# A delta-rule walk that deals its side work unevenly over the levels of each inverse

## The chip, the core and the metric

One core of a Trainium2 chip runs the whole program. Its five engines, TensorE (PE), VectorE (DVE), ScalarE (ACT), GpSimd (POOL) and SyncE (SP), each take their own instructions in the order in which the program issued them, and wait for one another on semaphores. The metric is device time in microseconds (us); lower is better.

## The reference

The program computes four blocks on 8 sequences of 512 tokens of width 256; two of them (a normalised linear attention, and a grouped attention with a mixture of experts) come in a later part of the program, and the tree-routed feed-forward partly so. The change touches only the first block, a gated delta rule with 8 heads, key width 128 and value width 64:

```python
def step(state, inp):
    q_t, k_t, v_t, a_t, b_t = inp
    retained = jnp.einsum('bhvk,bhk->bhv', state, k_t)
    a4 = a_t[..., None, None]
    b4 = b_t[..., None, None]
    rk = retained[..., None] * k_t[:, :, None, :]
    vk = v_t[..., None] * k_t[:, :, None, :]
    state = a4 * (state - b4 * rk) + b4 * vk
    o_t = jnp.einsum('bhvk,bhk->bhv', state, q_t)
    return (state, o_t)
...
q = _causal_dw_conv_silu(x @ Wq, conv_q).reshape(bsz, seq_len, H, KD)
k = _causal_dw_conv_silu(x @ Wk, conv_k).reshape(bsz, seq_len, H, KD)
v = _causal_dw_conv_silu(x @ Wv, conv_v).reshape(bsz, seq_len, H, VD)
q = _l2norm(q)
k = _l2norm(k)
...
_, outT = jax.lax.scan(step, state0, (qT, kT, vT, aT, bT))
...
out = out * rms * o_norm_w * jax.nn.silu(gate)
```

Instead of 512 steps one after another, the kernel works on chunks of 128 tokens. The steps inside a chunk amount to the inverse of a unit triangular 128x128 matrix for each head; the state is then carried from chunk to chunk.

## The kernel before

**Calls and inversions.** The stage `Delta` has 16 calls (`CALLS`): 8 sequences, and for each of them two groups of 4 heads. A call n has four chunks t = 0 to 3. Their inverses are made in two pairs, `invert(e, n, 0)` for chunks 0 and 1, and `invert(e, n, 1)` for chunks 2 and 3. That gives 32 inversions, m = 2n + pair; below an *even* inversion is the first of a call and an *odd* one the second.

**The generators.** Each engine walks the same list of generators. Each `yield` ends a step, and a step may issue nothing on an engine.

- `invert` has 30 steps, called M0 to M29 here. M0 to M5 are the set-up: PE makes K·K and K·Q (L708, L717), DVE scales them with the decays (L759, L764), DVE and ACT cut out the diagonal blocks (L901, L850), and DVE makes the first block inverse (L906, L909, L911). Then come six levels of 4 steps each, M6 to M29. In a level, PE makes the product T (L796; L798 in level 5; L820 with the transposes L824 in level 6). ACT copies it to SBUF (TB, L857). PE makes Z from it (L809; L834 in level 6). DVE merges Z into the inverse (L919) and transposes it (L921), and only then can the next T start. In level 6, DVE copies the results out (L929, L933). T stands at M6, M10, M14, M18, M22 and M26, Z two steps behind each, the copies TB at M7, M11, M15, M19, M23, M27, and L919 at M9, M13, M17, M21. From level 3 on PE also gets products that nobody reads, L841, one or two in each gap.
- `project` has 50 steps, p0 to p49, and works for the next call. Ten items (v for two halves, then k and q for four heads) stand at p2, p4, ..., p20 on PE: two fp32 matmuls of 512 columns (L570; the profile lists each as two records). One step later ACT copies the first tap of the convolution (L615), and another step later DVE adds the other three taps (L663, three instructions). Two Silu (L620) follow on ACT at p7, p11, p15, p19 and p23. Items alternate between two PSUM banks, so item j on PE waits for the three taps of item j - 2. p22 and p24 make the gate (L579 on PE, L625 on ACT; the second waits for the Silu of the first), p26 and p28 turn v (L589, L630), p30 to p44 turn k and q (L599 on PE, squares L641 on ACT, L669 on DVE).
- `state` carries the state over two chunks, 6 steps each: QS (L968 and L970 on PE), then L1004 to L1011 on DVE, then Uh (L977), L1015, O1 (L984 and L986), L1020 and L1021. The second pair adds 6 steps that normalise the output (L1026 to L1034 on DVE, a square root L1046 on ACT, L1063 and L1068 on POOL). `last` is the state of the previous call's second pair, `here` that of this call's first.
- `beside` is the routing of the feed-forward: small steps on all engines (L1282 to L1480) that share the walk.

**The dealing.** `side_by_side` issues one step of the inverse, and then as many steps of each other generator as its rate has added up to:

```python
def side_by_side(main, *others):
    due = [0.0] * len(others)
    for _ in main:
        for j, (steps, rate) in enumerate(others):
            due[j] += rate
            while due[j] >= 1:
                next(steps, None)
                due[j] -= 1
```

The rates are numbers written by hand in `walk`. `(next(main) for _ in range(6))` covers the set-up, and the bare `main` that follows covers all six levels. ACT has one table for Exp, one for Silu and one for Sqrt; where another function is wanted, an ACT_TABLE_LOAD goes ahead.

## Time and profile before

| | us |
|---|---|
| median of 3 runs | 3632.18 (3629.6 to 3633.38) |
| the profiled execution, time | 3636.05 |
| its span | 3634.3 |
| of it before the first inversion | 145 |
| from the first inversion's start to its last product | 1666 |
| PE busy in the span | 3184.9 (88%) |
| mean granted TensorE clock | 0.914 |

The span is from the first instruction of the profile to the last. The time of the profiled execution is 1.75 us longer than its span and 3.87 us above the median. A granted clock of 1.00 is the upper of TensorE's two levels (2.4 GHz) and 0.50 the lower (1.2 GHz), so a mean of 0.9 over a stretch says that a fifth of it was at the lower one.

### The profile page before, as it was taken

The numbers are of one execution on the slowest core, as the hardware profiler recorded it, in microseconds if no ns is written. First come the engines' busy times: TensorE is split into PE (matmuls) and PEld (weight loads), VectorE is DVE, ScalarE is ACT, GpSimd is POOL, SyncE is SP. The second block draws the span as 40 slices with busy tenths as digits, with TensorE's granted clock in tenths as the row PEclk, the third lists the DMA queues.
The fourth block names the chain that finished last, engine by engine and source line by source line (L and its number), as shares of the span: only waits on it lengthen the run. The fifth ranks groups of instructions, "written<-read, shape, count | busy, mean of one in ns | idle before, by whom it ended". The sixth has DMA issues, their size and how long they took to land.

```text
span 3634.3 us, 86956 instructions
## 1 busy us (share of the span) xinstructions
PE 3184.9 (88%) x35518; PEld 2222.1 (61%) x35518; DVE 2190.0 (60%) x4820; ACT 1428.4 (39%) x3328; POOL 933.8 (26%) x851
## 2 busy tenths in 40 slices
PE   5689988888998888888868889776999999999998
PEld 5366766666766666666757767665545554554553
DVE  6566778666678676678346645635445545545444
ACT  1544444444444444344136622134433433433341
POOL 0112231412222412221405536331221221220110
PEclk7799988899898999998679999988989999999999
DMA  6101211302111301111347755384111111111000
GB/s 239 41 34 49 65 48 34 126 27 65 54 47 49 120 26 50 60 54 32 101 152 198 188 161 145 102 276 157 24 43 45 47 35 47 40 31 41 1 18 18
DMA packets 224087, 280.89 MB, mean 77 GB/s; under 512 B 35072, under 2 KB 172464, under 8 KB 223312
## 3 DMA queue, kind: packets, MB, share of 16 engines
q1 hardware_dynamic: 184448, 216.93, 18.5%
q0 software_dynamic: 34896, 54.20, 6.7%
q8 instruction: 288, 4.72, 0.5%
q10 hardware_dynamic: 4352, 4.20, 0.3%
q14 instruction: 103, 0.84, 0.1%
HBM read 184.64 MB, written 90.62 MB: 76 GB/s over the span
## 4 chain that ended last, share of the span: by engine, by line
PE 68%; DVE 16%; ACT 5%; issue 4%; DMA 3%; POOL 1%; DVEq 0%; ACTq 0%; SPq 0%; POOLq 0%
PE banks L3024 6%; PE banks L570 5%; DVE s_d_kq L663 3%; PE banks L2590 3%; PE banks L809 3%; PE banks L2574 2%; PE banks L1940 2%; PE banks L1282 2%; PE banks L1949 2%; PE banks L796 2%; PE banks L2602 2%; PE banks L970 2%; PE banks L2832 2%; PE banks L968 2%; PE banks L2742 2%
## 5 line engine op out<-in xcount | busy, mean ns | idle before, releaser
L570 PE MATMUL banks<-s_d_xT,s_w_qkvg 128*128 128x512 f32 x640 | 349.1, 674 | 14.7 <-DVE s_d_kq L663 9.5
L663 DVE SCALAR_TENSOR_TENSOR s_d_kq<-banks,s_conv_w,s_d_kq 128x511 f32<-128x511 f32 (+2 forms) x384 | 286.0, 745 | 51.2 <-ACT s_d_kq L615 41.6
L2704 ACT ACTIVATE s_g_pT<-banks 128x1536 f32<-128x1536 f32 (+1 forms) x96 | 152.8, 1591 | 359.7 <-PE banks L2592 359.7
L2668 DVE TENSOR_REDUCE s_g_nmax<-banks 128x4 f32<-128x512 f32 (+3 forms) x128 | 188.0, 1490 | 161.2 <-PE banks L2576 161.2
L3024 PE MATMUL banks<-s_m_we,s_m_tT 128*128 128x512 f32 x512 | 233.9, 602 | 8.5 <-DVE s_m_x L3088 8.2
L641 ACT ACTIVATE s_d_square<-banks 128x128 bf16<-128x128 f32 x512 | 134.1, 276 | 168.6 <-PE banks L599 168.5
L570 PEld LDWEIGHTS banks<-s_d_xT,s_w_qkvg 128*128 128x128 f32 x640 | 126.7, 212 | 118.6 <-issue 91.2
L615 ACT ACTIVATE s_d_kq<-banks,s_conv_w 128x512 f32<-128x512 f32 x128 | 87.8, 686 | 275.6 <-PE banks L570 274.9
L1940 PE MATMUL banks<-s_q_xsT,s_q_w 128*128 x1008 | 159.1, 281 | 37.4 <-issue 28.2
L1940 PEld LDWEIGHTS banks<-s_q_xsT,s_q_w 128*128 128x128 f32 x1008 | 153.0, 195 | 59.5 <-issue 47.6
L796 PEld LDWEIGHTS banks<-s_d_Xc,s_d_Mc 32*32 32x32 f32 x8192 | 94.4, 117 | 125.4 <-DVE s_d_Xc L909 55.8
L809 PE MATMUL banks<-s_d_TB,s_d_XT 32*32 32x32 f32 x9216 | 131.0, 203 | 40.2 <-ACT s_d_TB L857 37.7
L796 PE MATMUL banks<-s_d_Xc,s_d_Mc 32*32 32x32 f32 x8192 | 110.4, 206 | 63.4 <-DVE s_d_Xc L909 48.9
L809 PEld LDWEIGHTS banks<-s_d_TB,s_d_XT 32*32 32x32 f32 x9216 | 111.7, 115 | 88.0 <-issue 42.4
L3024 PEld LDWEIGHTS banks<-s_m_we,s_m_tT 128*128 128x128 f32 x512 | 93.5, 192 | 112.9 <-issue 99.5
L1949 PE MATMUL banks<-s_q_w,s_q_hm 128*128 (+1 forms) x504 | 157.5, 395 | 3.6 <-DVE s_q_hm L2000 2.9
L1215 POOL DMA_INDIRECT s_r_bias<-b,s_r_leafi x96 | 94.3, 982 | 201.7 <-DMA tree<-s_r_bias 95.8
L2000 DVE SCALAR_TENSOR_TENSOR s_q_hm<-s_q_lrow,s_q_w,s_q_hT 128x128 f32<-128x128 f32 x252 | 86.6, 344 | 93.0 <-ACT s_q_hT L1970 78.5
L1970 ACT ACTIVATE s_q_hT<-banks,s_q_w 128x128 f32<-128x128 f32 x252 | 92.2, 366 | 118.0 <-PE banks L1940 115.3
L919 DVE COPY_PREDICATED s_d_Xc<-c_mask,banks 128x256 f32<-128x256 uint32 x128 | 56.4, 441 | 131.3 <-PE banks L809 131.3
L2029 POOL DMA_INDIRECT tree<-s_q_acc,s_q_toki x64 | 102.3, 1599 | 111.2 <-DVE s_q_acc L2009 94.7
L3086 DVE SCALAR_TENSOR_TENSOR s_m_x<-banks,s_m_comb,s_m_x 128x256 f32<-128x256 f32 x128 | 61.8, 483 | 108.0 <-PE banks L3024 105.7
(411 smaller groups left out, 7620.9 us busy)
## 6 DMA issues: line engine op xcount, KB each, us to landing
s_q_w<-w12p SPq DMA_DIRECT2D x128, 257.0 KB, 5.9
s_q_xs<-xs SPq DMA_DIRECT2D x32, 516.0 KB, 5.6
s_d_E<-sums SPq DMA_DIRECT2D x64, 256.0 KB, 3.5
s_r_xT<-xfT SPq DMA_DIRECT2D x12, 1024.0 KB
tree<-s_r_bias SPq DMA_DIRECT2D x96, 128.0 KB, 2.6
s_r_work<-xf SPq DMA_DIRECT2D x24, 512.0 KB, 4.1
og<-s_d_o SPq DMA_DIRECT2D x16, 512.0 KB, 3.0
sorted<-s_q_acc SPq DMA_DIRECT2D x32, 256.0 KB, 2.1
```

The source lines that it names most:

```text
L570: ins = e.matmul(bk[6 + j % 2][:], w[:, par, c, self.COL[what] + h * P:self.COL[what] + (h + 1) * P], xT[:, c, :], start=(c == 0), stop=(c ...
L641: ins = e.activation(self.square[:, k, h, :], bk[7 - k][:, h * P:(h + 1) * P], ACT.Square, accum_out=self.sums[:, k, H * t + h:H * t + h + 1])
L663: e.scalar_tensor_tensor(d[:, a:], bk[6 + j % 2][:, 0:SEQ - a], cw[:, par, k0 + 3 - a:k0 + 4 - a], d[:, a:], ALU.mult, ALU.add).then_inc(s ...
L796: ins = e.matmul(bk[0][r, 32 * a:32 * a + 32], Mc[r, a, :], Xc[r, a, :], start=True, stop=True)
L809: ins = e.matmul(bk[2][r, 32 * a:32 * a + 32], XT[r, a, :], TB[r, a, :], start=True, stop=True)
L1940: ins = e.matmul(bk[Q % 3][:, 0:P], self.w1[Q % self.COPIES][:, c * P:(c + 1) * P], tiles[:, c, ds(at[Q], 1), :], start=(c == 0), stop=(c ...
L1949: e.matmul(bk[3 + q % 3][:, 0:DIM], self.hm[q % 4][:], self.w12[:, ds(self.group(q, at[q]), 1), 258:], start=True, stop=True).then_inc(sel ...
L2029: e.indirect_dma_start(self.g.dram[f"tree{F}"], bass.IndirectOffsetOnAxis(self.toki[F % 2][:, t:t + 1].bitcast(U32), 0), self.acc[:, t * D ...
L2590: ins = e.matmul(bk[k][:, a:a + SEQ - c * P], qkT[32 * k:32 * k + 17, 4, c * P:(c + 1) * P], qkT[32 * k:32 * k + 17, j, c * P:SEQ], start= ...
L2668: e.tensor_reduce(self.nmax[:, t, :].rearrange("p (k d) -> p k d", k=4)[:, :, 16], psum[:, 0:4, a:a + (t + 1) * P], AX.X, ALU.max, negate= ...
L2704: e.activation(self.pT[c][:], psum[:, 0:4, 0:self.COLUMNS[c]], ACT.Exp).then_inc(self.exped, 1)
L3024: ins = e.matmul(bk[q][:], tT[:, c, t * P:(t + 1) * P], self.we[:, c, (2 * half + q) * 512:(2 * half + q + 1) * 512], start=(c == 0), stop ...
```

## The change

The six levels are split after the third. In an even inversion `last` gets 0.9 of a step per step of the inverse in levels 1 to 3 and 0.4 in levels 4 to 6 (0.64 throughout before), and `ahead`, the next projections, 0.5 and then 1.2 (0.8 throughout before). In an odd inversion `here` gets 0.7 and then 0.35 (0.5 before), and `ahead` 0.5 and 1.2 (0.8 before). Neither `beside` nor the set-up changes its rate.

```diff
             main, here = invert(e, n, 0), state(e, n, 0)
             side_by_side((next(main) for _ in range(6)), (last, 0.5), (ahead, 0.67))
-            side_by_side(main, (last, 0.64), (ahead, 0.8), (beside, 0.62))
+            side_by_side((next(main) for _ in range(12)), (last, 0.9), (ahead, 0.5), (beside, 0.62))
+            side_by_side(main, (last, 0.4), (ahead, 1.2), (beside, 0.62))
             finish(last)
             main = invert(e, n, 1)
             side_by_side((next(main) for _ in range(6)), (ahead, 1.34))
-            side_by_side(main, (here, 0.5), (ahead, 0.8), (beside, 0.62))
+            side_by_side((next(main) for _ in range(12)), (here, 0.7), (ahead, 0.5), (beside, 0.62))
+            side_by_side(main, (here, 0.35), (ahead, 1.2), (beside, 0.62))
             finish(here, ahead)
```

In levels 1 to 3 of an even inversion stood project's p4 to p12 and steps 3 to 9 of `last`; now p4 to p9 and steps 3 to 12. In levels 4 to 6 stood p13 to p22 and the rest of `last`; now p10 to p23 and steps 13 to 16. The last item that has its taps added ahead of L933 was p20's; now it is p22's. An odd inversion starts one step of `project` later, at p24. All engines keep the same instructions but for ACT's table loads: the program has 46 of them at L620 before and 32 after. The changed file has two lines more ahead of the routing, so that L1282 is L1284 there.

ScalarE, levels 1 to 3 of the even inversion m = 18; L857 is the copy TB that the next Z waits for, L615 a first tap, L620 a Silu. Before:

```order
L857 ACTIVATE s_d_TB<-banks 128x256
L615 ACTIVATE s_d_vT<-banks,s_conv_w 128x512
L615 ACTIVATE s_d_kq<-banks,s_conv_w 128x512
L620 ACT_TABLE_LOAD
L620 ACTIVATE s_d_vT<-s_d_vT 128x512 x2
L857 ACTIVATE s_d_TB<-banks 128x256
L615 ACTIVATE s_d_kq<-banks,s_conv_w 128x512
L857 ACTIVATE s_d_TB<-banks 128x256
```

After:

```order
L857 ACTIVATE s_d_TB<-banks 128x256
L615 ACTIVATE s_d_vT<-banks,s_conv_w 128x512
L857 ACTIVATE s_d_TB<-banks 128x256
L615 ACTIVATE s_d_kq<-banks,s_conv_w 128x512
L620 ACT_TABLE_LOAD
L620 ACTIVATE s_d_vT<-s_d_vT 128x512 x2
L857 ACTIVATE s_d_TB<-banks 128x256
L615 ACTIVATE s_d_kq<-banks,s_conv_w 128x512
```

The first tap of item 2, the table load and the Silu of v stood ahead of level 2's copy and now stand behind it.

TensorE at the same place, from the T of level 2 (L796) to the T of level 3; L809 is Z, L968 with L970 is QS, L977 is Uh, L570 an item. Before:

```order
L796 MATMUL banks<-s_d_Xc,s_d_Mc 32x32 x32
L809 MATMUL banks<-s_d_TB,s_d_XT 32x32 x32
L968 MATMUL banks<-s_d_S,s_d_kq 128x64 x4
L970 MATMUL banks<-s_d_S,s_d_kq 128x64 x4
L570 MATMUL banks<-s_d_xT,s_w_qkvg 128x512 x2
L796 MATMUL banks<-s_d_Xc,s_d_Mc 32x32 x32
```

After:

```order
L796 MATMUL banks<-s_d_Xc,s_d_Mc 32x32 x32
L968 MATMUL banks<-s_d_S,s_d_kq 128x64 x4
L970 MATMUL banks<-s_d_S,s_d_kq 128x64 x4
L570 MATMUL banks<-s_d_xT,s_w_qkvg 128x512 x2
L809 MATMUL banks<-s_d_TB,s_d_XT 32x32 x32
L977 MATMUL banks<-s_d_R,s_d_Pf 128x64 x4
L796 MATMUL banks<-s_d_Xc,s_d_Mc 32x32 x32
```

Between T and Z of level 2 stood nothing; QS and an item now stand there, and only Uh stands behind Z.

VectorE at the end of level 6 of the same inversion; L663 are the taps (three instructions to an item), L929 and L933 copy the finished inverse, and L933 lets PE go on with the next set-up. Before:

```order
L929 COPY s_d_Pf<-banks 128x512
L663 SCALAR_TENSOR_TENSOR s_d_kq<-banks,s_conv_w,s_d_kq 128x511
L663 SCALAR_TENSOR_TENSOR s_d_kq<-banks,s_conv_w,s_d_kq 128x510
L663 SCALAR_TENSOR_TENSOR s_d_kq<-banks,s_conv_w,s_d_kq 128x509
L1394 TENSOR_SCALAR s_r_posi<-s_r_pos 128x32
L933 COPY s_d_Pf<-banks 64x8x64
```

After:

```order
L929 COPY s_d_Pf<-banks 128x512
L663 SCALAR_TENSOR_TENSOR s_d_kq<-banks,s_conv_w,s_d_kq 128x511
L663 SCALAR_TENSOR_TENSOR s_d_kq<-banks,s_conv_w,s_d_kq 128x510
L663 SCALAR_TENSOR_TENSOR s_d_kq<-banks,s_conv_w,s_d_kq 128x509
L1393 TENSOR_REDUCE s_r_pos<-s_r_work 128x32
L663 SCALAR_TENSOR_TENSOR s_d_kq<-banks,s_conv_w,s_d_kq 128x511
L663 SCALAR_TENSOR_TENSOR s_d_kq<-banks,s_conv_w,s_d_kq 128x510
L663 SCALAR_TENSOR_TENSOR s_d_kq<-banks,s_conv_w,s_d_kq 128x509
L933 COPY s_d_Pf<-banks 64x8x64
```

The taps of the last item moved from behind L933 to ahead of it. From level 3's L919 to L933 DVE has the taps of seven items now, and had those of five.

## Rows read from the trace of the kernel before

**Rows 1.** The page: its first line and the first of part 1.
```profile
span 3634.3 us, 86956 instructions
...
PE 3184.9 (88%) x35518; PEld 2222.1 (61%) x35518; DVE 2190.0 (60%) x4820; ACT 1428.4 (39%) x3328; POOL 933.8 (26%) x851
```

**Rows 2.** Busy time by stretch: the delta stage (stretch, length, engines, clock, DMA).
```profile
145.00:1811.00 1666.00, 1473.00 (x24880) 1106.38 (x24879) 1158.56 (x2462) 712.64 (x1953) 448.00 (x430) 0.89 0.19 57
```

**Rows 3.** Waits of PE in the delta stage: waiter, releaser, total us, times, longest.
```profile
PE banks L796 <- DVE s_d_Xc L909: 48.9, 32, 7.4
PE banks L809 <- ACT s_d_TB L857: 37.7, 16, 2.8
PE banks L977 <- DVE s_d_T L1008: 25.7, 39, 2.2
...
PE banks L798 <- DVE s_d_Xc L919: 15.8, 12, 2.9
```

**Rows 4.** Timeline of PE, m = 10: start, us, instruction [idle before, releaser].
```profile
688.00 0.80 PE L796 MATMUL banks<-s_d_Xc,s_d_Mc 32*32 32x32 f32 x64
691.57 0.65 PE L809 MATMUL banks<-s_d_TB,s_d_XT 32*32 32x32 f32 x52 [2.78 <-ACT s_d_TB L857]
...
695.92 3.73 PE L570 MATMUL banks<-s_d_xT,s_w_qkvg 128*128 128x512 f32 x4
699.58 1.01 PE L796 MATMUL banks<-s_d_Xc,s_d_Mc 32*32 32x32 f32 x64
...
704.40 1.88 PE L570 MATMUL banks<-s_d_xT,s_w_qkvg 128*128 128x512 f32 x4
...
706.89 1.10 PE L984 MATMUL banks<-s_d_U,s_d_kdec 128*128 128x64 f32 x8
707.84 1.06 PE L986 MATMUL banks<-s_d_U,s_d_DD 128*128 128x64 f32 x8
```

**Rows 5.** Timeline of ACT at the same place.
```profile
688.10 0.69 ACT L615 ACTIVATE s_d_kq<-banks,s_conv_w 128x512 f32<-128x512 f32 x1 [4.11 <-PE banks L570]
688.81 1.28 ACT L620 ACT_TABLE_LOAD   x1
690.10 1.15 ACT L620 ACTIVATE s_d_vT<-s_d_vT 128x512 f32<-128x512 f32 x2
691.16 0.36 ACT L857 ACTIVATE s_d_TB<-banks 128x256 f32<-128x256 f32 x1
```

**Rows 6.** Busy time by stretch: levels 1-3 and 4-6 of m = 10, 18, 16, 13.
```profile
680.60:706.20 25.60, 22.02 (x446) 14.16 (x446) 16.55 (x33) 7.25 (x12) 11.09 (x12) 0.87 0.41 137
706.20:725.70 19.50, 18.99 (x282) 12.31 (x282) 16.90 (x28) 16.17 (x25) 4.59 (x3) 1.00 0.10 30
...
1094.50:1118.90 24.40, 21.77 (x446) 13.99 (x446) 18.95 (x40) 7.25 (x12) 6.61 (x7) 0.86 0.17 52
1118.90:1143.40 24.50, 21.14 (x283) 12.82 (x283) 23.96 (x38) 16.28 (x25) 6.40 (x4) 0.93 0.13 36
...
998.40:1022.40 24.00, 23.86 (x470) 16.55 (x470) 17.78 (x35) 7.25 (x12) 5.23 (x6) 1.00 0.13 40
1022.40:1042.10 19.70, 19.13 (x283) 12.36 (x283) 18.13 (x36) 16.17 (x25) 7.57 (x6) 1.00 0.15 47
...
846.90:860.60 13.70, 11.92 (x442) 10.46 (x442) 8.28 (x19) 6.85 (x43) 7.14 (x8) 1.00 0.36 114
860.60:876.50 15.90, 14.15 (x293) 11.97 (x293) 9.52 (x27) 10.77 (x37) 1.27 (x2) 1.00 0.23 73
```

**Rows 7.** Timeline of DVE in m = 10.
```profile
693.09 0.44 DVE L919 COPY_PREDICATED s_d_Xc<-c_mask,banks 128x256 f32<-128x256 uint32 x1 [1.94 <-PE banks L809]
...
705.13 4.50 DVE L663 SCALAR_TENSOR_TENSOR s_d_kq<-banks,s_conv_w,s_d_kq 128x511 f32<-128x511 f32 x6
...
721.37 2.31 DVE L663 SCALAR_TENSOR_TENSOR s_d_kq<-banks,s_conv_w,s_d_kq 128x511 f32<-128x511 f32 x3
724.03 0.68 DVE L933 COPY s_d_Pf<-banks 64x512 f32<-64x512 f32 x1 [0.34 <-PE banks L834]
```

## The prediction, made before the changed kernel ran

> **What bounds the kernel now.** First the page: TensorE is busy for 88% of the span, VectorE for 60% [rows 1]. The change touches one stage only, so the next view is the busy time of that stretch: 1666 us, of which PE is busy 1473 and idle 193, at a mean granted clock of 0.89 [rows 2]. With levels of 1.0 and 0.5 this means 0.11 / 0.5 x 1666 = 366 us at the lower one, which cost up to 183 us. So PE's order bounds the stage, and there are two things to win in it: waits, and the half clock that follows them. PE's waits tell where they are [rows 3]: 48.9 us before the first level, which the change doesn't touch; 37.7 us in 16 waits before Z (L809) for the copy TB on ACT; and smaller ones in the state (L977) and before level 5 (L798).
>
> The timelines show the second of these in full. In m = 10 the T of level 2 is done at 688.80, and Z starts at 691.57 after an idle of 2.78 [rows 4]. On ACT the copy could have run at 688.8, but it is queued behind a first tap, a table load and two Silu and starts at 691.16 [rows 5]. Behind the wait, the same item that takes 1.88 us elsewhere takes 3.73, and T 1.01 [rows 4]: the array is at its lower clock. The stretch of levels 1 to 3 has a mean of 0.87, that is 0.13 / 0.5 x 25.6 = 6.7 us at half clock, or 3.3 us lost [rows 6]. Of the 14 even inversions m = 2 to 28, 12 look like this one; m = 4 and 16 don't, since routing products fill the gap (clock 1.00 in m = 16, [rows 6]). Odd inversions have no such place (13.7 and 15.9 us in m = 13, clock 1.00 [rows 6]).
>
> The Trainium skill says the same of the clock (TensorE: Matmul & The Clock Gate, "HAM oscillation"): a long wait sends the array back to half rate, and the work behind it pays. By that rule, the trace agrees; whether smaller waits in a row do it too is a rival below.
>
> **Levels 1 to 3, even.** (a) Level 2's copy now stands ahead of the first tap, load and Silu, and PE has QS and an item between T and Z. The wait of 2.78 goes; the item hides the copy, which needs 0.36 [rows 5]. If that cover failed, the copy alone would cost some 0.5. **-2.8.** (b) With no such wait the 6.7 us at the lower clock go: **-3.3.** (c) Five items become three, 2 x 1.83 us [rows 4], **-3.7**, and one O1 (L984 and L986, 706.89 to 708.73, [rows 4]) comes in, **+1.85**. (d) What is late next: T of level 3. Its L919 on DVE stands behind L1004 to L1011 (about 1.5 us), which wait for QS, and behind item 1's taps, half of 4.50 = 2.25 us [rows 7]. From QS's end that is some 4.2 us, with an item, Z and Uh (1.83 + 0.7 + 0.93) on PE beside it: a wait of 0.8 to 1.0, and 0.35 more before level 4. **+1.4.** Sum **-6.5** in an inversion like m = 10.
>
> Where routing steps keep DVE busy, (d) grows. In m = 18 DVE is busy 18.95 of 24.40 us [rows 6]. Following its order through gives 1.0 before level 2's T, 1.0 before level 3's and 0.5 elsewhere: +2.5 in place of 1.4. Sum **-5.4**. In m = 4 and 16, (a) and (b) have nothing to win: about **-1**.
>
> **Levels 4 to 6, even.** Here the change gives back. PE gets two items and loses an O1, +1.8. DVE has seven trios of taps between L919 of level 3 and L933 where it had five, and loses the two additions of the state: 2 x 2.25 - 0.75 = +3.75. In m = 10 DVE is busy 16.90 of 19.50 us [rows 6]; with 20.65 of work it becomes the bound. Since item j + 2 on PE waits for item j's taps, and taps for ACT's first tap, it can't run without gaps. Worked through, it waits about 1 us before item 6's taps (ACT has the Exp load and the Sqrt load ahead of them) and about 1 us for items 8 and 9. That is 22.8 against 19.5: **+3.3**. The last trio, which stood behind L933 [rows 7], stands ahead of it, and L933 releases the next set-up; that is in this number. In m = 18 DVE is at 23.96 of 24.50 already [rows 6]: waits close up, but everything added shows, **+3.0**. Bounds: PE's +1.8 alone, if DVE keeps up, to +5.5, two trios and both loads in the open. I take the middle, since rows of m = 10 and m = 18 give the same from either end.
>
> One table load of 1.28 us [rows 5] leaves each of 14 even inversions: Silu's table is still there for items 2 and 3. Worth nothing early, where ACT has room; in the late half it is in the +3.3.
>
> In the trace a Silu starts at 690.10, right when the load of 688.81 ends [rows 5]. The Trainium skill (ScalarE: Activation LUTs, "What ACT_TABLE_LOAD costs") adds a drain of 1.38 us to each load; no such gap is here. By its 2.66 us the removed load would be worth up to 1.4 us more in each light inversion, and the estimate for the change some 8 us lower.
>
> **Odd inversions.** The work is the same; QS moves from the late half into level 3, Uh and O1 one gap forward. m = 13 takes 29.6 us with 26.1 of PE [rows 6]: 3.5 of waits. In the new order I find 0.85 before level 2's T (L1004 to L1011 ahead of L919), 0.9 before level 5's Z (ACT: squares, Exp load, squares) and 1.25 before level 6's T: 3.0. **-0.5** each, with bounds of -2 (part of the half clock goes, since large products now fill levels 2 and 3) and +1 (the waits fall where nothing covers them).
>
> **The sum.** Six light even inversions with the stall (m = 2, 10, 14, 20, 26, 28): 6 x (-6.5 + 3.3) = -19. Six busy ones (6, 8, 12, 18, 22, 24): 6 x (-5.4 + 3.0) = -14. Two without: 2 x (-1 + 3) = +4. Half clock behind the new waits in the busy ones, PE not being the bound there: +3. Odd: 15 x -0.5 = -8. The first call -1; the last has no `ahead` and its tail is bound by latency, 0. Together -35 us, on the profiled execution's 3636.05: 3601. That execution was 3.87 above the median, so the forecast is 3632.2 - 35 = **3597**. Its own range: late half at +1.8 in twelve (-18) and odd at -1 (-8) give 3571; late half at +4.5 (+16) and odd at +0.5 (+15) give 3628.
>
> **Rivals.** (1) *The late half takes it all back.* DVE is near its limit there (23.96 of 24.50 [rows 6]). If each late half grows by about 5.5, the gain of 12 x 6 = 72 meets 14 x 5.5 = 77, and with the odd ones' -8 and the two early -1 it ends within a few us of now: 3625 to 3639. For it: DVE rows of m = 18. Against: in m = 10 DVE has 2.6 us free, and early DVE work falls by the same 3.75.
>
> (2) *Slower: the half clock moves to levels 4 to 6.* There PE would wait for taps before items 6 to 9 and before level 5's T. If that drags the late half's clock to the 0.87 of today's early half [rows 6], 24 us at that mean lose 3.1; with the upper bound of +5.5 a late half grows by 8.6 against 6 won: +2.6 x 12, and +7.6 in each of the two without a stall, less 8 in the odd ones, is +38: about 3670; half of that clock loss gives 3652. It decides from about +6 us a late half. For it: before level 5, PE waits already in the present order (15.8 us, up to 2.9 [rows 3]). Against: these waits are of about 1 us, and PE isn't the bound while it waits.
>
> The Trainium skill has this as a rule (same page, "A second HAM failure mode": frequent short idles between groups of matmuls make the clock swing). The trace speaks against it so far: m = 13 has 3.5 us of scattered waits in 29.6 at clock 1.00 [rows 6].
>
> (3) *A larger gain.* Of 366 us at the lower clock only 12 x 6.7 = 80 stand behind the stall. If denser levels 2 and 3 lift another third of the rest, 95 / 2 = 48 us more go: 3549.
>
> (4) *The change does not do what it says.* The order of the built program shows the copy ahead of the load in all of these inversions; excluded.
>
> **How the numbers follow.** A measurement of this kernel can tell about 0.2%, 7.3 us, from no change. Forecast 0.65, nearly all of it faster by more than that; rival 1 0.14, rival 2 0.13, rival 3 0.08. So faster 0.72, same 0.15, slower 0.13. The range reaches from 3566 to 3638: it holds the forecast's own and rival 1, and leaves out rival 2 and nearly all of rival 3.
>
> **What would show it.** The wait of L809 for TB falls from 37.7 us to under 8, and the item behind level 2 takes 1.9. Levels 1 to 3 of m = 10 take about 19, levels 4 to 6 with the first set-up products about 3.3 more than now. New rows among PE's waits: L570 for L663, and T (L796, L798) for L919. The stage's clock rises from 0.89 to about 0.91 and its length falls to about 1631. What would make it wrong: a late half longer by 6 us or more, a clock under 0.95 in it where it is 1.00 now, or odd inversions longer than 30 us.

## The result, and the profile after

The changed kernel takes 3701.38 us (median of 4 runs, 3677.88 to 3713.22), against 3632.78 for the kernel before in the same comparison (3629.6 to 3635.42). The ratio is 1.0173 with a 95% interval of 1.0138 to 1.0207: **slower by 1.7%**, where a gain of 1% was forecast. The profiled execution took 3697.73 us, with a span of 3696.0 and a mean granted clock of 0.897 (0.914 before).

The head of the page after, with the first line of its part 1, answers to [rows 1]:

```profile
span 3696.0 us, 86942 instructions
...
PE 3252.0 (88%) x35518; PEld 2271.2 (61%) x35518; DVE 2184.1 (59%) x4820; ACT 1411.0 (38%) x3314; POOL 935.2 (25%) x851
```

PE has the same 35518 instructions and is busy 67 us longer. ACT has 14 instructions less, the table loads.

The busy time of the delta stage after (stretch, length, PE, PEld, DVE, ACT, POOL, clock, DMA share, GB/s) answers to [rows 2]:

```profile
149.00:1863.00 1714.00, 1525.92 (x24876) 1147.27 (x24875) 1153.08 (x2462) 695.13 (x1936) 450.74 (x430) 0.86 0.18 55
```

This line holds the result. The stage is 48 us longer. PE's idle time in it is 1714 - 1526 = 188 us, and was 193: **the waits did not grow** in their sum. The clock fell from 0.89 to 0.86, so the time at the lower level rose from 366 us to 0.14 / 0.5 x 1714 = 480. These 114 us lose 57, which is the stage's growth within the rounding of the clock. Of the other 14 us of span, 4 lie ahead of the stage and 10 behind it (3634.3 - 1811 = 1823 before, 1833 after); the kernels below take 1822 to 1836 behind it, whatever their dealing.

PE's waits in the stage after (waiter, releaser, total, times, longest) answer to [rows 3]; the wait for TB is from a window that ends at 1900:

```profile
PE banks L796 <- DVE s_d_Xc L909: 48.5, 32, 7.4
PE banks L796 <- DVE s_d_Xc L919: 39.1, 44, 2.2
PE banks L820 <- ACT s_d_X L867: 26.2, 15, 2.5
PE banks L798 <- DVE s_d_Xc L919: 20.0, 17, 2.6
...
PE banks L809 <- ACT s_d_TB L857: 1.6, 2, 1.1
```

The same view of before had two lines that the forecast didn't quote:

```profile
PE banks L820 <- ACT s_d_X L867: 19.1, 23, 3.1
...
PE banks L796 <- DVE s_d_Xc L919: 8.0, 20, 1.2
```

The wait for TB went, 37.7 to 1.6, as forecast. In its place stand 31 us more before T (L796) for L919, 4 more before L798 and 7 more before level 6's T (L820) for the copies of X.

Levels 1 to 3 and 4 to 6 of m = 10, 18, 16 and 13, in the columns of [rows 6]:

```profile
704.80:730.00 25.20, 21.41 (x454) 15.72 (x454) 14.42 (x29) 5.64 (x9) 12.96 (x13) 0.80 0.36 125
730.00:752.30 22.30, 21.27 (x274) 11.90 (x275) 19.99 (x31) 16.49 (x27) 2.70 (x2) 1.00 0.10 28
...
1148.90:1169.10 20.20, 18.82 (x454) 13.03 (x454) 16.36 (x36) 5.53 (x9) 6.59 (x6) 0.92 0.12 38
1169.10:1195.10 26.00, 23.26 (x275) 12.49 (x276) 24.95 (x39) 16.49 (x27) 6.58 (x6) 0.93 0.19 54
...
1044.10:1071.30 27.20, 25.46 (x478) 19.39 (x478) 14.88 (x32) 5.75 (x9) 7.36 (x8) 0.87 0.08 26
1071.30:1093.50 22.20, 21.10 (x273) 11.85 (x274) 20.86 (x38) 16.50 (x27) 5.41 (x5) 1.00 0.25 69
...
877.90:895.60 17.70, 15.19 (x454) 13.51 (x454) 8.47 (x23) 5.20 (x33) 7.15 (x8) 0.89 0.33 102
895.60:914.60 19.00, 16.64 (x282) 13.57 (x281) 8.23 (x23) 11.80 (x45) 3.20 (x3) 0.77 0.15 50
```

The late halves of the even ones cost 1.5 to 2.8 us more, at an unchanged clock. The early half of m = 18 won 4.2. But that of m = 10, forecast at about 19 us, went only from 25.6 to 25.2, with its clock at 0.80 instead of 0.87; m = 16, which had a clock of 1.00 and no stall, lost 3.2 in its early half at 0.87; and the odd m = 13 went from 29.6 us at 1.00 to 36.7, at 0.89 and 0.77.

I took the same sums over all inversions, from one set-up's first product to the next one's, with "half" for the us at the lower clock in them (the sum of (1 - clock) / 0.5 x length). Means over 14 even (m = 2 to 28) and 15 odd ones:

| us, mean | before | after |
|---|---|---|
| even: set-up (half) | 9.9 (0.3) | 10.7 (2.4) |
| even: levels 1 to 3 (half) | 25.6 (5.6) | 23.4 (5.4) |
| even: levels 4 to 6 (half) | 23.8 (2.3) | 25.3 (1.8) |
| odd: set-up | 9.3 | 9.5 |
| odd: levels 1 to 3 (half) | 17.1 (7.6) | 19.9 (10.1) |
| odd: levels 4 to 6 (half) | 19.0 (4.0) | 19.5 (7.8) |

The even ones sum to 59.3 before and 59.4 after, the odd ones to 45.4 and 48.9: 15 x 3.5 = 52 us, the whole loss of the stage. An odd inversion spends 18.1 us at the lower clock instead of 11.7 and loses 3.2 by it; its idle time grew from 5.3 to 6.1 in the mean, while that of an even one fell from 6.3 to 5.2.

PE in the odd m = 17 after (start, us, instruction, in brackets the idle before it and its releaser) shows where it comes from:

```profile
1102.98 0.75 PE L796 MATMUL banks<-s_d_Xc,s_d_Mc 32*32 32x32 f32 x64 [1.80 <-DVE s_d_Xc L909]
...
1108.18 0.75 PE L796 MATMUL banks<-s_d_Xc,s_d_Mc 32*32 32x32 f32 x64 [1.40 <-DVE s_d_Xc L919]
...
1111.42 1.97 PE L984 MATMUL banks<-s_d_U,s_d_kdec 128*128 128x64 f32 x8
...
1136.13 1.00 PE L984 MATMUL banks<-s_d_U,s_d_kdec 128*128 128x64 f32 x8
```

The T of level 1 waits 1.80 for the set-up, as it did before. Five us later the T of level 2 waits another 1.40. Two us behind the start of that T the products slow down (L984 takes 1.97, and 1.00 at the end). The lower clock lasts for 17 us, in all of which PE is busy:

```profile
1110.20:1127.30 17.10, 17.10 (x371) 14.52 (x369) 10.88 (x21) 5.70 (x28) 0.67 (x1) 0.50 0.01 3
1127.30:1136.10 8.80, 7.30 (x114) 5.53 (x115) 6.32 (x16) 7.05 (x33) 1.25 (x2) 1.00 0.39 121
```

m = 3, 5, 9, 19 and 21 are like it. Of the 13 odd inversions from m = 1 to 25, 11 fall to the lower clock in levels 1 to 3, for 4 to 19 us of them; in m = 1, 7, 15 and 23 they do so already behind the first wait.

The kernel before had this fall too, without a wait of level 2's T for L919: 8 of the same 13 inversions fall in levels 1 to 3, for 3 to 19 us. The forecast's stand-in, m = 13, is one of the five that don't. Levels 1 to 3 of m = 9 and 15 before:

```profile
633.30:653.60 20.30, 18.35 (x446) 16.04 (x449) 8.24 (x21) 6.75 (x43) 10.32 (x12) 0.55 0.43 140
948.00:967.70 19.70, 19.23 (x445) 16.63 (x445) 9.81 (x20) 6.65 (x43) 6.35 (x7) 0.54 0.41 128
```

In m = 13 after the change the second wait is 0.94, and its half clock starts only behind a pause of 1.29 us in level 3's Z for which the profile shows no releaser. The other new wait stands at level 6. PE in m = 13:

```profile
906.87 1.11 PE L820 MATMUL banks<-s_d_X,s_d_M 64*64 64x64 f32 x16 [2.36 <-ACT s_d_X L867]
907.91 1.14 PE L824 MATMUL banks<-c_ident,s_d_X 128*128 128x128 f32 x8
908.85 1.81 PE L984 MATMUL banks<-s_d_U,s_d_kdec 128*128 128x64 f32 x8
```

ACT ahead of this wait shows why it is so long:

```profile
902.37 0.39 ACT L857 ACTIVATE s_d_TB<-banks 128x256 f32<-128x256 f32 x1
902.78 0.84 ACT L887 ACTIVATE s_d_X<-s_d_Xc 32x256 f32<-32x256 f32 x2
903.64 0.28 ACT L641 ACTIVATE s_d_square<-banks 128x128 bf16<-128x128 f32 x1
...
905.96 0.76 ACT L867 ACTIVATE s_d_X<-banks 32x256 f32<-32x256 f32 x2
```

Between L887 and L867, the copies of X that level 6 needs, there are now eight squares (L641), two groups. Before there were four, one group.

In the even inversions the half clock didn't go, it moved. PE in m = 16, from the T of level 2 to the item of level 3:

```profile
1052.80 0.75 PE L796 MATMUL banks<-s_d_Xc,s_d_Mc 32*32 32x32 f32 x64
...
1057.10 1.88 PE L570 MATMUL banks<-s_d_xT,s_w_qkvg 128*128 128x512 f32 x4
1058.91 0.75 PE L809 MATMUL banks<-s_d_TB,s_d_XT 32*32 32x32 f32 x64
1059.59 1.11 PE L977 MATMUL banks<-s_d_R,s_d_Pf 128*128 128x64 f32 x8
1062.23 0.98 PE L796 MATMUL banks<-s_d_Xc,s_d_Mc 32*32 32x32 f32 x64 [1.53 <-DVE s_d_Xc L919]
1063.14 1.97 PE L984 MATMUL banks<-s_d_U,s_d_kdec 128*128 128x64 f32 x8
...
1067.03 2.99 PE L570 MATMUL banks<-s_d_xT,s_w_qkvg 128*128 128x512 f32 x4
```

Level 2's Z comes without a wait. The T of level 3 waits 1.53, and behind it the products run at the lower clock, the item at 2.99 for 1.88. Over the 14 even inversions this wait has a mean of 1.3 and is above 0.7 in 13. Before, 4.5 us of half clock in the mean stood behind level 2's Z; now 3.5 stand behind level 3's T.

### The profile page after: what moved, and what is told of

It reads as the page before. It is cut to its first block, busy times and chain, and to the rows that moved or that the text cites. A ratio compares the mean times of both kernels' runs of the same rounds, so it can differ in the third digit from the quotient of the medians.

```text
span 3696.0 us, 86942 instructions
## 1 busy us (share of the span) xinstructions
PE 3252.0 (88%) x35518; PEld 2271.2 (61%) x35518; DVE 2184.1 (59%) x4820; ACT 1411.0 (38%) x3314; POOL 935.2 (25%) x851
## 4 chain that ended last, share of the span: by engine, by line
PE 67%; DVE 17%; ACT 5%; issue 4%; DMA 3%; POOL 1%; DVEq 0%; ACTq 0%; SPq 0%; POOLq 0%
PE banks L3026 6%; DVE s_d_kq L663 4%; PE banks L570 4%; PE banks L2592 3%; PE banks L1284 2%; PE banks L1942 2%; PE banks L2576 2%; PE banks L984 2%; PE banks L796 2%; PE banks L1951 2%; PE banks L986 2%; PE banks L2604 2%; PE banks L809 2%; PE banks L968 2%; PE banks L2834 2%
## 5 line engine op out<-in xcount | busy, mean ns | idle before, releaser
L570 PE MATMUL banks<-s_d_xT,s_w_qkvg 128*128 128x512 f32 x640 | 342.2, 662 | 16.3 <-DVE s_d_kq L663 12.6
L663 DVE SCALAR_TENSOR_TENSOR s_d_kq<-banks,s_conv_w,s_d_kq 128x511 f32<-128x511 f32 (+2 forms) x384 | 286.3, 746 | 25.3 <-ACT s_d_kq L615 16.1
L2706 ACT ACTIVATE s_g_pT<-banks 128x1536 f32<-128x1536 f32 (+1 forms) x96 | 152.8, 1591 | 361.3 <-PE banks L2594 361.3
L2670 DVE TENSOR_REDUCE s_g_nmax<-banks 128x4 f32<-128x512 f32 (+3 forms) x128 | 188.0, 1490 | 161.9 <-PE banks L2578 161.9
L570 PEld LDWEIGHTS banks<-s_d_xT,s_w_qkvg 128*128 128x128 f32 x640 | 124.3, 207 | 128.5 <-issue 89.1
L857 ACT ACTIVATE s_d_TB<-banks 128x256 f32<-128x256 f32 x160 | 61.2, 382 | 344.1 <-PE banks L796 331.6
L1942 PEld LDWEIGHTS banks<-s_q_xsT,s_q_w 128*128 128x128 f32 x1008 | 154.1, 196 | 59.3 <-issue 47.1
L796 PE MATMUL banks<-s_d_Xc,s_d_Mc 32*32 32x32 f32 x8192 | 109.0, 206 | 90.0 <-DVE s_d_Xc L909 48.5
L809 PEld LDWEIGHTS banks<-s_d_TB,s_d_XT 32*32 32x32 f32 x9216 | 114.1, 117 | 89.6 <-issue 83.2
L615 ACT ACTIVATE s_d_kq<-banks,s_conv_w 128x512 f32<-128x512 f32 x128 | 87.5, 683 | 212.5 <-PE banks L570 212.0
L641 ACT ACTIVATE s_d_square<-banks 128x128 bf16<-128x128 f32 x512 | 133.8, 277 | 90.7 <-PE banks L599 90.2
L796 PEld LDWEIGHTS banks<-s_d_Xc,s_d_Mc 32*32 32x32 f32 x8192 | 93.4, 117 | 117.2 <-DVE s_d_Xc L909 55.4
L809 PE MATMUL banks<-s_d_TB,s_d_XT 32*32 32x32 f32 x9216 | 133.4, 206 | 7.1 <-issue 5.5
L841 PE MATMUL banks<-c_negmb,c_identb 128*128 128x512 bf16 x352 | 129.9, 431 | 0.0
```

The source lines that it names most:

```text
L570: ins = e.matmul(bk[6 + j % 2][:], w[:, par, c, self.COL[what] + h * P:self.COL[what] + (h + 1) * P], xT[:, c, :], start=(c == 0), stop=(c ...
L641: ins = e.activation(self.square[:, k, h, :], bk[7 - k][:, h * P:(h + 1) * P], ACT.Square, accum_out=self.sums[:, k, H * t + h:H * t + h + 1])
L663: e.scalar_tensor_tensor(d[:, a:], bk[6 + j % 2][:, 0:SEQ - a], cw[:, par, k0 + 3 - a:k0 + 4 - a], d[:, a:], ALU.mult, ALU.add).then_inc(s ...
L796: ins = e.matmul(bk[0][r, 32 * a:32 * a + 32], Mc[r, a, :], Xc[r, a, :], start=True, stop=True)
L809: ins = e.matmul(bk[2][r, 32 * a:32 * a + 32], XT[r, a, :], TB[r, a, :], start=True, stop=True)
L841: e.matmul(self.g.bank[3][:].rearrange("p (h n) -> p h n", h=H), self.g.identb[:], self.g.negm[:, None, :].broadcast_to((P, H, P)), start= ...
```

## The experiments

My theory, formed from these traces: the change costs by the clock alone; new short waits close to other waits send the array to its lower level, and products that fill those waits (unread ones, issued for that alone) give the time back. The rival: the loss is work and waits that were moved to a place where nothing covers them, and stays when the clock is held. Against the kernel before, ratios are given with their 95% intervals. Runs of the kernel before itself went from 3616 to 3658 us over all comparisons, so differences of some 15 us between two kernels are at the edge of what these runs tell.

### One half of the change alone

**e1_even**: only the even inversions are dealt anew.

```diff
-            side_by_side((next(main) for _ in range(12)), (here, 0.7), (ahead, 0.5), (beside, 0.62))
-            side_by_side(main, (here, 0.35), (ahead, 1.2), (beside, 0.62))
+            side_by_side(main, (here, 0.5), (ahead, 0.8), (beside, 0.62))
```

> Only the even inversions are dealt anew; odd ones keep 0.5 and 0.8. Theory A (the loss is half clock in the odd inversions: they grew by 3.5 us each, even ones by nothing): no slower than before, about 3620, between 3605 and 3635; waits of L809 for L857 nearly gone. Theory B (the longer late half of the even inversions, with its seven trios of taps, is what costs): 3660 or more, with the odd inversions at their old length.

Measured: 3630.63 us, ratio 0.9979 (0.9952 to 1.0006), no difference. The stage's line:

```profile
145.00:1811.00 1666.00, 1469.55 (x24879) 1099.24 (x24879) 1155.15 (x2462) 694.97 (x1936) 449.46 (x430) 0.89 0.19 57
```

The same 1666 us and 0.89 as before, though the wait for TB is all but gone (1.6 us): T waits 33.4 us for L919 instead, 8.0 before. (This profiled execution took 3649 us, 13 more than that of the kernel before, and all of it lies behind the stage.) The even dealing trades one wait for another, each with its half clock. L820 waits only 6.3 us for L867 here.

**e2_odd**: only the odd inversions are dealt anew.

```diff
-            side_by_side((next(main) for _ in range(12)), (last, 0.9), (ahead, 0.5), (beside, 0.62))
-            side_by_side(main, (last, 0.4), (ahead, 1.2), (beside, 0.62))
+            side_by_side(main, (last, 0.64), (ahead, 0.8), (beside, 0.62))
```

> Only the odd inversions are dealt anew; even ones keep 0.64 and 0.8. Theory A: about 3632 + 15 x 3.5 = 3685, between 3665 and 3700, with the stage's clock at 0.87 or below. Theory B: within 10 us of 3632, since the even inversions stay as they were.

Measured: 3673.19 us, ratio 1.0113 (1.0053 to 1.0173). An odd inversion takes 46.6 us with 14.2 at half clock, an even one 59.8. The loss sits in the odd part. It is smaller than the whole change's; the odd inversion starts at p23 here: one group of squares stands ahead of L867 and one behind it, and level 6's T waits 1.1 us in the mean, not 1.7. The two parts interact: the even dealing takes one more step of `project`, and that pushes the second group of squares ahead of L867.

**e7_odd_state** and **e8_odd_ahead** split the odd part again, on the kernel before: only `here` is dealt anew, or only `ahead`.

```diff
# e7_odd_state
-            side_by_side(main, (here, 0.5), (ahead, 0.8), (beside, 0.62))
+            side_by_side((next(main) for _ in range(12)), (here, 0.7), (ahead, 0.8), (beside, 0.62))
+            side_by_side(main, (here, 0.35), (ahead, 0.8), (beside, 0.62))
# e8_odd_ahead
-            side_by_side(main, (here, 0.5), (ahead, 0.8), (beside, 0.62))
+            side_by_side((next(main) for _ in range(12)), (here, 0.5), (ahead, 0.5), (beside, 0.62))
+            side_by_side(main, (here, 0.5), (ahead, 1.2), (beside, 0.62))
```

> The kernel before, with only the state's rates of the odd inversions changed (0.7 and 0.35); the projections stay at 0.8. The changed odd inversion puts L1004 to L1011 ahead of L919 on VectorE (new wait before level 2's T) and keeps both groups of squares ahead of the copies of X on ScalarE only through the projections. If the state's dealing makes the wait before level 2: that wait is there (over 0.6 us in most odd inversions), the one before level 6 stays at 0.9, and the time is 3640 to 3665.

> The kernel before, with only the projections' rates of the odd inversions changed (0.5 and 1.2); the state stays at 0.5. If the projections' dealing makes the wait before level 6 (two groups of squares ahead of the copies of X): that wait is over 1.5 us, the one before level 2's T is near nothing, and the time is 3640 to 3665. If this half of the dealing is harmless: 3625 to 3638.

Measured: 3634.31 (ratio 0.9997, 0.997 to 1.0024) and 3639.1 (1.001, 0.9982 to 1.0038). Neither costs anything that can be told. For the first I had expected a loss, and for the second either a loss with over 1.5 us of wait before level 6 or none. In e7_odd_state the wait before level 2's T is there (1.1 us), and with it 12.5 us at half clock in levels 1 to 3, where the kernel before has 7.6. These levels take 21.0 us for 17.1, which is 3.9 more. But the late half falls from 19.0 to 15.0 us: level 6's T no longer waits (0.02), and half clock there is 1.5 for 4.0. So the state's part has the cost that the theory gives it, and wins as much back elsewhere. In e8_odd_ahead level 6's T waits 0.4, level 2's not at all, and levels 1 to 3 stay at 17.2. By their ratios the two parts alone give -1 and +4 us, and together (e2_odd) +41, 19 to 63 by its interval. With both, levels 1 to 3 take 19.6 and the late half 17.5, since level 6's T waits 1.1 again: the early loss stays, and the gain that went with it is mostly gone. e7_odd_state has nearly as much half clock in an odd inversion as e2_odd (14.1 and 14.2) and is 1.3 us shorter, 0.9 of it idle time. So the clock alone doesn't explain the step between these two.

### Products in the waits

`L841`, the product that nobody reads, writes a bank that is free there; it changes no output. The following kernels issue more of them. `AHEAD` products stand ahead of level 1's T, behind a wait for the set-up's K·K result; `UNREAD_T` and `UNREAD_Z` give the number behind T and Z. The first tuple is for even inversions, the second for odd ones; its first entry isn't used, and the others are levels 1 to 5. The lines in these kernels are six higher: L796, L820, L841, L867, L909, L919, L968 and L977 are L802, L826, L847, L873, L915, L925, L974 and L983.

**e3_after_fill**, the changed kernel:

```diff
-    UNREAD = (0, 0, 0, 1, 2, 2)
+    AHEAD = (4, 8)
+    UNREAD_T = ((0, 0, 0, 1, 2, 2), (0, 0, 0, 1, 2, 2))
+    UNREAD_Z = ((0, 0, 4, 1, 2, 2), (0, 4, 0, 1, 2, 8))
```

Four products stand ahead of level 1's T in even inversions and eight in odd ones. Four more fill the wait before level 3's T (even) and the one before level 2's T (odd), and six more the one before level 6's T (odd).

> The changed kernel, with unread products (L841's kind, 0.21 us each) put into the places where PE waits: 4 (even) and 8 (odd) ahead of level 1's T, 4 behind Z of level 1 (odd), 4 behind Z of level 2 (even), 6 more behind Z of level 5 (odd). No result depends on them. Theory A: the work fits the waits, the clock of the delta stage rises from 0.86 to over 0.91 and the time falls to 3630 or less. Rival C (the waits and the order of real work set the time, and the clock is only a symptom): 29 us of products come in, some of them too long for their wait, and the time is 3701 or more.

**e4_before_fill**, the same three tables on the kernel before, tells what they are worth without the change.

> The kernel before, with the same unread products. Theory A: in the old order the waits before level 1 (48.9 us in all) and before level 6 are filled too, while the 2.8 us before level 2's Z in the even inversions is not: clock 0.91 to 0.93 and 3590 to 3620. Rival C: 3632 to 3655.

Measured: e3_after_fill 3559.74 us, ratio **0.9796** (0.9756 to 0.9836); e4_before_fill 3620.92, ratio 0.9965 (0.9946 to 0.9984). The stage of the first and of the second:

```profile
141.00:1729.00 1588.00, 1466.29 (x25290) 1055.60 (x25290) 1153.16 (x2462) 695.94 (x1936) 452.96 (x430) 0.96 0.19 60
```
```profile
145.00:1786.00 1641.00, 1489.57 (x25292) 1080.98 (x25290) 1159.75 (x2462) 714.65 (x1949) 449.09 (x430) 0.94 0.19 58
```

On the changed kernel 416 more products make PE 60 us *less* busy, since the clock is 0.96. Half clock falls from 480 us to 0.04 / 0.5 x 1588 = 127, and the stage from 1714 to 1588. m = 13 in this kernel:

```profile
809.80:823.80 14.00, 13.96 (x458) 12.11 (x458) 8.44 (x23) 5.25 (x33) 6.99 (x8) 1.00 0.38 109
823.80:839.90 16.10, 14.36 (x288) 11.03 (x287) 8.42 (x23) 11.82 (x45) 2.08 (x3) 1.00 0.25 78
```

30.1 us, where the changed kernel took 36.7. And PE before level 6 of it:

```profile
831.79 1.90 PE L847 MATMUL banks<-c_negmb,c_identb 128*128 128x512 bf16 x8
...
834.85 1.11 PE L826 MATMUL banks<-s_d_X,s_d_M 64*64 64x64 f32 x16 [1.16 <-ACT s_d_X L873]
```

Eight products take 1.90 us of the wait, 1.16 are left, and the clock stays up.

On the kernel before the same tables bring 0.35% only, a little less than I expected: its 37.7 us of waits for TB are untouched, with their half clock. So with these products in both kernels, the changed order is ahead by 3620.92 - 3559.74 = **61 us**, where its measured effect without them was +69. Of the 53 us by which the two stages differ, 35 are still clock (half clock 197 against 127 us), and PE is idle for 29 less (151 against 122); the two sum to more, within the rounding of the clock and the other work. The rival would keep the changed kernel behind the kernel before; it falls.

The comparison isn't even-handed: the tables are made for the waits of the new order. In the old one the four products behind Z of level 2 (even) and of level 1 (odd) stand where the next T waits for L919 for 0.1 us or less in the mean, and the 2.8 us before level 2's Z stay empty. A kernel before with products in its own waits wasn't run, so it isn't shown how much of the 61 us the order itself is worth.

**e11_even_fill**, e1_even with the same tables, divides the 61 us.

> Only the even inversions dealt anew, with the unread products of e3_after_fill in both kinds. It tells whether the odd inversions' new dealing is worth anything once the clock is held: e3_after_fill took 42.8 us for an odd inversion and the old dealing with the same products 43.7 (e4_before_fill). If that difference is real: 3565 to 3585, some 14 us more than e3_after_fill. If it is not: 3555 to 3565.

Measured: 3593.02 us, ratio 0.9892 (0.9844 to 0.9939), longer than both of the ranges that I had expected. With these products, the even dealing is worth about 3620.9 - 3593.0 = 28 us and the odd one about 3593.0 - 3559.7 = 33; the interval of this run is 35 us wide, so the division is rough.

### Which products do it

**e5_fill_ahead** has only those ahead of level 1's T, **e6_fill_behind** only those in the waits that the change made.

```diff
# e5_fill_ahead
-    UNREAD_Z = ((0, 0, 4, 1, 2, 2), (0, 4, 0, 1, 2, 8))
+    UNREAD_Z = ((0, 0, 0, 1, 2, 2), (0, 0, 0, 1, 2, 2))
# e6_fill_behind
-    AHEAD = (4, 8)
+    AHEAD = (0, 0)
```

> The changed kernel, with the unread products only ahead of level 1's T (4 in even, 8 in odd inversions), where both orders wait about as long. If the clock falls because this wait and the new one behind Z of level 1 come close together, filling the first is enough for levels 1 to 3: half clock there under 4 us an odd inversion (10.1 in the changed kernel), but the 3.9 us in level 6 stay. Time 3620 to 3660. If the new waits alone are to blame, 3690 or more.

> The changed kernel, with the unread products only in the waits that the change made (4 behind Z of level 1 and 6 more behind Z of level 5 in odd inversions, 4 behind Z of level 2 in even ones). If the new waits alone are to blame: 3600 or less. If the first wait of an inversion counts as well: half clock of level 6 gone, that of levels 1 to 3 partly there, 3620 to 3660.

Measured: 3645.93 us (ratio 1.0021, 0.9989 to 1.0052) and 3569.05 (0.9802, 0.9751 to 0.9854). Each helps: against the changed kernel's 3701, the first 55 us, the second 132. The second nearly equals both together. The second came out as if the new waits alone were to blame (3600 or less); its half clock in the odd levels 1 to 3, 3.9 us, says that the first wait counts as well. In e6_fill_behind the wait of level 1's T is all there (48.6 us in 32 waits), and an odd inversion still has only 4.4 us at half clock, for 18.1 in the changed kernel. That wait still brings the clock down in some inversions, but fewer (8 of the 13 from m = 1 to 25, for 11) and for a shorter time, 3 to 14 us. m = 17 there:

```profile
1018.01 0.75 PE L802 MATMUL banks<-s_d_Xc,s_d_Mc 32*32 32x32 f32 x64 [1.80 <-DVE s_d_Xc L915]
1018.69 1.87 PE L974 MATMUL banks<-s_d_S,s_d_kq 128*128 128x64 f32 x8
...
1024.07 1.81 PE L847 MATMUL banks<-c_negmb,c_identb 128*128 128x512 bf16 x4
1025.81 0.75 PE L802 MATMUL banks<-s_d_Xc,s_d_Mc 32*32 32x32 f32 x64
1026.49 1.10 PE L983 MATMUL banks<-s_d_R,s_d_Pf 128*128 128x64 f32 x8
```

L974 (the changed kernel's L968) doubles right behind the 1.80. The four products take the place of the second wait, and at their end PE is back at the upper clock, 7 us after it fell, where the changed kernel stays low for 17. **A second wait close behind the first makes the lower clock last longer.** e6_fill_behind alone doesn't show it, since its four products also put work there. But the kernels without products say the same. Half clock in the odd levels 1 to 3 is 7.6, 7.4 and 8.1 us where level 2's T hardly waits for L919 (before, e1_even, e8_odd_ahead), and 10.1, 10.1 and 12.5 where it does (after, e2_odd, e7_odd_state). That it falls more often isn't shown: 8, 11 and 11 of the 13 against 11, 9 and 12. e5_fill_ahead shows it from the other side: with the first of the pair filled and the second not, half clock in these levels falls from 10.1 to 5.1 us, a little above the 4 I had expected, while level 6's, whose wait isn't filled, stays (5.3 in the changed kernel, 6.9 here).

**e10_fill_elsewhere** has the same number of products as e3_after_fill, 8 and 18 more to an inversion, at places where PE hardly waits.

```diff
-    AHEAD = (4, 8)
-    UNREAD_T = ((0, 0, 0, 1, 2, 2), (0, 0, 0, 1, 2, 2))
-    UNREAD_Z = ((0, 0, 4, 1, 2, 2), (0, 4, 0, 1, 2, 8))
+    AHEAD = (0, 0)
+    UNREAD_T = ((0, 2, 0, 3, 4, 2), (0, 4, 0, 5, 6, 3))
+    UNREAD_Z = ((0, 0, 0, 3, 2, 2), (0, 0, 0, 4, 4, 2))
```

> The changed kernel with as many unread products as e3_after_fill (8 more in an even, 18 more in an odd inversion), but at places where TensorE hardly waits: behind T of levels 1, 3, 4 and 5, and behind Z of levels 3 and 4. If what counts is the filled waits: no better than the changed kernel, 3690 to 3760 (26 products of 0.21 us in 16 calls are 87 us of work, part of it hidden). If more TensorE work anywhere keeps the clock up: 3640 or less.

Measured: 3686.18 us, ratio 1.0127 (1.008 to 1.0174). Its stage, and two of its waits:

```profile
143.00:1878.00 1735.00, 1562.55 (x25292) 1146.30 (x25290) 1154.57 (x2462) 696.27 (x1934) 448.10 (x430) 0.90 0.18 55
```
```profile
PE banks L802 <- DVE s_d_Xc L925: 35.0, 35, 2.6
...
PE banks L826 <- ACT s_d_X L873: 23.5, 16, 1.7
```

The profiled execution was one of its longer ones (span 3710.9). Half clock is down to 0.10 / 0.5 x 1735 = 347 us, but the new waits stand and the products are mostly added work: PE is busy 1563 us, not 1466. The place is worth 3686 - 3560 = 126 us. The number alone is worth the 15 us to 3701 at most, which these runs can't tell from nothing.

### More products

**e9_fill_more** fills further, **e12_fill_mid** adds a few in the middle.

```diff
# e9_fill_more
+    AHEAD = (6, 11)
+    UNREAD_Z = ((0, 2, 5, 1, 6, 2), (0, 6, 0, 1, 2, 10))
# e12_fill_mid
+    AHEAD = (4, 8)
+    UNREAD_Z = ((0, 0, 4, 1, 6, 2), (0, 5, 0, 1, 2, 9))
```

> The changed kernel with more unread products in the waits that are left in e3_after_fill: 6 and 11 ahead of level 1's T, 2 and 6 behind Z of level 1, 5 behind Z of level 2 (even), 6 behind Z of level 4 (even), 10 behind Z of level 5 (odd). Theory A: half clock in the stage under 133 us, time 3540 to 3560. If the places are full by now, the added products push real work back: 3560 to 3580.

> The changed kernel with e3_after_fill's products and one more behind Z of levels 1 and 5 (odd), four more behind Z of level 4 (even), where 1.3 us of wait were left. Theory A: half clock of the stage between e3_after_fill's 133 and e9_fill_more's 84 us, time 3550 to 3565.

Measured: 3566.62 us (ratio 0.9806, 0.9759 to 0.9853) and 3570.92 (0.9836, 0.9786 to 0.9886). e9_fill_more has the highest clock of all, 0.97 in the stage, and PE busy for 1496 us where e3_after_fill has 1466: what the clock gives, the added products take. Neither is better than e3_after_fill within the intervals. For e12_fill_mid I had expected 3550 to 3565. e3_after_fill is the best version found, 2% faster than the kernel before.

### All stages beside one another

"Half" is (1 - clock) / 0.5 x stage, good to about 17 us since the clock has two digits. The stages are those of the profiled executions, the medians those of all.

| kernel | stage | PE busy | idle | half | median |
|---|---|---|---|---|---|
| before | 1666 | 1473 | 193 | 366 | 3632.18 |
| after | 1714 | 1526 | 188 | 480 | 3701.38 |
| e1_even | 1666 | 1470 | 196 | 366 | 3630.63 |
| e2_odd | 1690 | 1499 | 191 | 439 | 3673.19 |
| e7_odd_state | 1670 | 1487 | 183 | 434 | 3634.31 |
| e8_odd_ahead | 1666 | 1466 | 200 | 367 | 3639.1 |
| e4_before_fill | 1641 | 1490 | 151 | 197 | 3620.92 |
| e5_fill_ahead | 1683 | 1531 | 152 | 404 | 3645.93 |
| e6_fill_behind | 1594 | 1438 | 156 | 159 | 3569.05 |
| e3_after_fill | 1588 | 1466 | 122 | 127 | 3559.74 |
| e11_even_fill | 1619 | 1477 | 142 | 162 | 3593.02 |
| e12_fill_mid | 1592 | 1482 | 110 | 127 | 3570.92 |
| e9_fill_more | 1591 | 1496 | 95 | 95 | 3566.62 |
| e10_fill_elsewhere | 1735 | 1563 | 172 | 347 | 3686.18 |

The first four have the same idle time within 8 us and the same work, and differ by the half clock: 114 us more of it in the changed kernel, 48 longer; 73 more in e2_odd, 24 longer. e7_odd_state doesn't fall in line as well: 68 more and only 4 longer, of which the 10 us less of idle time and the rounding explain a part.

## Why the prediction was wrong

**What bounds the kernel.** Two steps failed: term (b), by which the half clock goes with the stall, and the term for the odd inversions, which had no clock in it. The even inversions were forecast at -27 us together and came out at +2; the odd ones at -8, and came out at +52. What was right: PE's order bounds the stage, and waits and the half clock behind them are the two things to win. The weight was wrong. I looked at waits one by one and at the clock only behind the stall of 2.78 us, though 366 us stood at the lower level and 80 of them behind that stall.

**Levels 1 to 3, even: term (b) failed.** (a) and (c) came as forecast: the wait for TB is gone, the item hides the copy. (d) named the right place, T of level 3 behind L919, and its size was about right (0.8 to 1.0 forecast, where its own rows give 0.7; 1.3 measured). But (b), -3.3, took it for granted that "with no such wait the 6.7 us at the lower clock go". They moved behind the wait of (d): half clock in the early half was 5.6 and is 5.4. The mean gain is 2.3 us instead of 5.2 (six times 6.5, six times 5.4, two times 1, by 14). Of the two inversions without a stall, forecast at -1, m = 16 lost 3.2 for the same reason.

**Levels 4 to 6, even: over-sized.** +3.3 and +3.0 were forecast; m = 10 measured +2.8, m = 18 +1.5, the mean +1.5. The clock didn't suffer. That DVE took the added taps with fewer gaps on PE than I worked out is likely, but no run separates it.

**Odd inversions: the term that decided, and wrong in sign.** Forecast -0.5 each with bounds of -2 and +1, measured +3.5. The waits themselves were not far off: 0.85 forecast before level 2's T and 1.1 measured, 1.25 before level 6's T and 1.7 measured. The latter came short because I put the second group of squares behind L867, where the built order has it ahead. That is 0.7 us of wait. (The 0.9 before level 5's Z didn't come.) The rest, 3.2 us, is half clock, 18.1 us in place of 11.7, and the forecast's upper bound had no clock in it. m = 13, at 1.00, was one of the undisturbed ones and a poor stand-in for the mean, which already had 11.7 us at half clock; the trace of the kernel before could have told, with 8 of 13 odd inversions at the lower clock behind the wait of 1.8.

**The rivals.** Rival 2 had the mechanism (the half clock moves to new, smaller waits) and the sign, and was short in size (3652 to 3670 against 3701; worked through again, its lower end is 3649). It put it in levels 4 to 6 of the even inversions, where the clock stayed at 1.00 in m = 10 and 16 and at 0.93 in m = 18, as before. Rival 1's even part came true in its result, 59.3 against 59.4 us, but not by the late half. Rival 3's idea, that a clock held up is worth more than the waits themselves, is what e3_after_fill shows, only that it needed products in the new waits. The argument against rival 2 was that a wait of about 1 us does nothing, from m = 13 with its 3.5 us of scattered waits at clock 1.00. The runs show that what such a wait costs hangs on what stands close to it. Where level 2's wait is added behind level 1's (before to e7_odd_state), half clock in levels 1 to 3 grows by 4.9 us; where level 1's is taken from ahead of it (after to e5_fill_ahead), it shrinks by 5.0.

The Trainium skill's rule that I set aside there (TensorE: Matmul & The Clock Gate, "A second HAM failure mode") says of one kernel, which cycles through PSUM banks, that short idles between groups of matmuls make the clock swing and cost throughput. The trace after agrees: in m = 17 the clock is 0.50 for 17 us behind waits of 1.80 and 1.40, and the stage's falls from 0.89 to 0.86 with 193 and 188 us of idle time.

**The sum.** -35 us was forecast for the order of instructions. With the clock mostly held by products in the new waits (e4_before_fill to e3_after_fill) the difference is -61. That has the forecast's sign, but it holds what the products do for the new order and not for the old one, so it doesn't confirm the working of waits and work. Without the products, the change measured +69.

**Left open.** The two parts of the odd dealing each cost nothing alone and 41 us together (e2_odd against e7_odd_state and e8_odd_ahead). The wait before level 6 explains a part: between the profiled stages of e2_odd and e7_odd_state lie 20 us, between their medians 39, and the rest is open. What products in the old order's own waits would give is open too. Nor is it known why the same wait of 1.8 us brings the clock down in one inversion and not in the next. And 122 us of idle time and some 130 of half clock remain in e3_after_fill.

## What to carry to other kernels

When work is moved to take away a wait on TensorE, follow the order to the next waits and ask of each what stands close to it: the half clock that a stall had caused goes only if no new wait takes its place. Read idle time and clock as two accounts; here the first was unchanged and the second made the result. Where a wait can't be avoided, a few products that nobody reads, in exactly that place, can turn a loss into a gain (3701 to 3560 us), while the same number at places without a wait brings next to nothing (3686). And before one inversion stands for all, look whether it is like the mean: m = 13 was at the upper clock where 8 of 13 were not.

## What the hardware showed that I had not expected

- Waits of 1.5 to 1.8 us can lower the granted clock. One of 1.8 does it in 8 of 13 odd inversions of the kernel before, for 3 to 19 us of levels 1 to 3, and not in the other five; where most have a second of 0.6 to 2.2 some 5 us later (e7_odd_state), half clock there rose from 7.6 to 12.5 us in the mean.
- The lower clock can outlast its cause by far: in m = 17 it lasts for 17 us in which PE is never idle, and in the even inversions 2.4 us of it reach into the set-up from the inversion ahead.
- Adding 416 matmuls where TensorE had waited made its busy time in the stage fall from 1526 to 1466 us.
- The kernel before varies by 1.2% between runs (3616 to 3658 us, 19 of them), and the granted clock of these runs with it (0.921 in the shortest, 0.907 in the longest).
